# An attention stage rewritten: head products in pairs of 32-row tiles, one ring of bank pairs, the exp mask on GpSimd, head means out of the weights

## The chip, the core and the metric

The kernel runs on one core of a Trainium2 chip. The metric is the device time of one execution in microseconds: before, a median of 3298.95 over three runs (3294.93 to 3305.66). Times in the text are us unless marked ns.

## The reference

Four layers over x of 4 batches × 1,024 tokens × 128: causal attention, a mixture of experts, a message layer (sigmoid of products, 16 channels), and the same mixture again. Only attention is changed. Cut to it:

```python
x = x + attention(layernorm(x))                 # b, t, e = 4, 1024, 128; 16 heads of s = 8
k, q, v = (z @ Wk), (z @ Wq), (z @ Wv)          # each to (b, t, 16, 8)
k = layernorm(k over s) * kln_w + kln_b         # q likewise, with qln_w, qln_b
dot = einsum('bqhs,bkhs->bhqk', q, k) / sqrt(8)
dot = where(causal, dot, -inf)
out = einsum('bhqk,bkhs->bqhs', softmax(dot), v).reshape(b, t, e)
attention = out @ Wo + bo
```

## The kernel before

Phases follow each other with a barrier between: `setup_phase`, `attention_phase`, `moe_phase`, `message_phase`, `moe_phase`. In attention a **group** is 4 heads of one batch; 4 groups a batch, 16 in all. Tokens stand in 8 tiles of 128. Each head has a stack of 32 rows (`STACK`): high part of q or k, low part, high part again, and two rows for the shift by the row's maximum. Four stacks make 128 rows. `q_st` and `k_st` hold them by token; TensorE transposes them (L367) to `qT`, `kT`, `qmT` with tokens along the free dimension. Since one product must see one head only, `kT` has a copy of 1,024 columns for each head with zeros in the other heads' rows (`spread_keys`, L816 on VectorE for the first half, L577 on ScalarE for the second), and every product runs over all 128 rows.

A group does two passes over its scores. **Maxima** (one group ahead): TensorE makes q·k for a tile of queries (L390), adds the causal mask with a product of identity and mask (L393) into one of four 512-column banks `unit`, and VectorE reduces it (L823), 43 units a group. Then the **shift** (L831 to L835) puts minus the maximum into `q_st`, which is transposed again to `qmT`. **Scores**: for a tile j of keys, TensorE makes k·q shifted (L413), adds the mask (L416) into one of two banks `score`, and ScalarE takes exp into `prob` (L616), 43 units a group. **Weighing**: one step j behind, the values times `prob` go to `o_acc` (L435), fp32, in four 32-column tiles, one a head, side by side. After step 7 ScalarE copies `o_acc` to `oT` (L605), TensorE transposes it back (L449), VectorE divides by the sums (L845, L846). At a batch's end come the transposes of `o_tok`, the product with Wo (L532), and the addition to x (L922, L924, L929).

While one batch's groups run, the next batch is prepared: token statistics (L685), z (L695), its transposes, projection (L381), copies on ScalarE (L560, L561), means of heads, centring, squares, variance, scaling, weight and bias (L715 to L743) and stacks (L747 to L804) on VectorE.

The order is written out by hand in `program`: scores of step j, `beside` places maxima units between them by `max_slice`, then weighing of step j - 1. TensorE executes in that order. Two counters run for the banks, one for `score`, one for `unit`; a unit is filled when the unit before it in the same bank has been emptied:

```python
def wait_empty(self, eng):
    eng.wait_ge(unit_free[self.n % BANKS], self.b * (UNITS_BATCH // BANKS) + self.n // BANKS + 1)
```

Batch 0 is prepared ahead of the loop, the loop `Fori` runs batches 0 to 2, and the last batch stands behind it. GpSimd only clears buffers in this stage; SyncE clears rows in DRAM for the next stage.

## Time and profile before

| | |
|---|---|
| median of 3 runs | 3298.95 |
| profiled execution | 3302.05 |
| its span, instructions | 3300.3, 58108 |
| TensorE busy, weight loads | 2977.8, 1822.9 |
| VectorE, ScalarE, GpSimd | 1919.3, 1469.5, 546.5 |
| attention: first score product, last copy of `o_acc`, last statistics | 104.3, 894.4, 904.2 |
| longest waits from 104 to 900: ScalarE's exp for the mask product L416 | 178.0 |
| the same, for the score product L413 | 77.4 |
| TensorE's weight load of a score for ScalarE's exp | 86.5 |

The span is that of one execution. Busy time counts an instruction from start to end; TensorE's products overlap, so their busy time holds the tails of the last ones, and the distance from one start to the next tells what one costs in a row. "PEld" is the load of the stationary operand. "L413" is a line of the kernel; a helper's line stands for all its calls.

### The profile page before, as it was taken

The page shows a single profiled execution, that of the slowest core. Times are in us where ns is not written, and L with a number is a line of the kernel's source. Part 1 is how long each engine was busy: PE and PEld are TensorE (multiplying, and loading weights), DVE is VectorE, ACT ScalarE, POOL GpSimd, SP SyncE. Part 2 cuts the span into 40 slices and gives each one's busy share as a digit, 9 for nine tenths or more (in the row PEclk, how much of TensorE's full clock was granted, in tenths as well). Part 3 has the DMA queues.
Part 4 walks back from the last instruction along what each step waited for, and adds up shares of the span by engine and source line. Part 5 has one row for each costly group of instructions (what it writes and reads, how often), then busy time and mean ns, then how long its engine had stood idle before and what let it go on. Part 6 is the DMA issues. An engine that isn't in the chain of part 4 may idle for free. (4 is left out here: it accounts for less than half of the span.)

```text
span 3300.3 us, 58108 instructions
## 1 busy us (share of the span) xinstructions
PE 2977.8 (90%) x19154; PEld 1822.9 (55%) x19155; DVE 1919.3 (58%) x3658; ACT 1469.5 (45%) x2438; POOL 546.5 (17%) x577
## 2 busy tenths in 40 slices
PE   2898998989868995999999999999999999966997
PEld 1455555555466883555555555555555555545886
DVE  5696776866356674545455555555455544546666
ACT  1455555555544443444444444444444444424443
POOL 1000000000065431111111111111111111135732
PEclk8998998999968997999999999999999999976999
DMA  9000000000032313888888888888888888842222
GB/s 159 1 1 2 1 1 2 1 1 1 6 97 62 87 40 98 198 198 201 199 189 196 201 200 196 193 197 200 195 200 194 198 195 200 199 119 75 64 69 79
DMA packets 202940, 389.02 MB, mean 118 GB/s; under 512 B 44562, under 2 KB 117147, under 8 KB 198555
## 3 DMA queue, kind: packets, MB, share of 16 engines
q1 hardware_dynamic: 193562, 367.95, 48.4%
q0 software_dynamic: 9216, 19.02, 1.7%
q8 instruction: 88, 1.44, 0.2%
q14 instruction: 74, 0.60, 0.1%
HBM read 35.23 MB, written 31.75 MB: 20 GB/s over the span
## 5 line engine op out<-in xcount | busy, mean ns | idle before, releaser
L2019 DVE STREAM_TRANSPOSE m_turned<-m_sig 128x1024 f32<-128x1024 f32 x512 | 613.1, 1226 | 597.2 <-ACT m_sig L1932 576.2
L1932 ACT ACTIVATE m_sig<-m_f_ps 128x1024 f32<-128x1024 f32 x512 | 496.4, 1021 | 609.2 <-PE m_f_ps L1804 609.2
L1817 PE MATMUL m_v_ps<-m_sig,m_tok 128*64 128x512 f32 x2048 | 497.0, 606 | 0.0
L1829 PE MATMUL m_v_ps<-m_sigT,m_tok 128*64 128x256 f32 x4096 | 465.8, 380 | 7.5 <-DMA m_sigT<-m_turned 7.4
L616 ACT ACTIVATE a_prob<-a_score 128x512 f32<-128x512 f32 (+3 forms) x688 | 346.1, 528 | 263.8 <-PE a_score L416 178.0
L1804 PE MATMUL m_f_ps<-m_swap,m_own 64*128 64x512 f32 x1536 | 442.8, 421 | 12.0 <-DMA m_swap<-m_own 9.8
L1804 PE MATMUL m_f_ps<-m_own,m_swap 64*128 64x512 f32 x1536 | 442.9, 421 | 0.0
L823 DVE TENSOR_REDUCE a_maxima<-a_unit 128x1 f32<-128x512 f32 (+5 forms) x688 | 373.9, 597 | 95.2 <-PE a_unit L393 67.5
L1829 PEld LDWEIGHTS m_v_ps<-m_sigT,m_tok 128*64 128x64 f32 x4096 | 293.6, 137 | 213.3 <-issue 71.2
L413 PE MATMUL a_score<-a_qmT,a_kT 128*128 128x512 f32 (+3 forms) x768 | 315.7, 436 | 44.4 <-ACT a_prob L616 26.3
L1804 PEld LDWEIGHTS m_f_ps<-m_swap,m_own 64*128 64x128 f32 x1536 | 270.5, 186 | 142.8 <-issue 86.1
L390 PE MATMUL a_unit<-a_kT,a_qT 128*128 128x512 f32 (+3 forms) x768 | 289.7, 412 | 15.7 <-issue 4.6
L1956 POOL TENSOR_TENSOR m_own<-m_uv,m_own 128x1024 fp32r<-128x1024 f32 x64 | 152.1, 2377 | 842.9 <-ACT m_own L1917 842.9
L1804 PEld LDWEIGHTS m_f_ps<-m_own,m_swap 64*128 64x128 f32 x1536 | 270.3, 186 | 3.6
L1817 PEld LDWEIGHTS m_v_ps<-m_sig,m_tok 128*64 128x64 f32 x2048 | 124.4, 136 | 239.7 <-issue 239.7
L413 PEld LDWEIGHTS a_score<-a_qmT,a_kT 128*128 128x128 f32 x768 | 153.5, 202 | 128.0 <-ACT a_prob L616 86.5
L1393 POOL TENSOR_SCALAR f_h<-x,f_mean,f_rstd 128x128 f32<-128x128 f32 x64 | 50.2, 802 | 911.0 <-DVE f_away L1550 911.0
L1405 POOL DMA_INDIRECT back_rows<-f_y_rows,f_goes_to x160 | 154.6, 966 | 244.5 <-DVE f_y_rows L1581 236.4
L390 PEld LDWEIGHTS a_unit<-a_kT,a_qT 128*128 128x128 f32 x768 | 154.4, 204 | 69.9 <-issue 41.3
L1922 ACT COPY m_tok<-m_unit 128x512 f32<-128x512 f32 x128 | 69.0, 590 | 250.1 <-PE m_unit L1788 250.1
L1251 PE MATMUL f_y_ps<-f_w_down,f_innerT 128*128 x1280 | 169.5, 275 | 1.7 <-DVE f_y_rows L1581 1.3
L2028 DVE COPY m_v1T<-m_v_ps 128x256 f32<-128x256 f32 x128 | 54.3, 424 | 194.4 <-PE m_v_ps L1829 194.0
(286 smaller groups left out, 4279.7 us busy)
## 6 DMA issues: line engine op xcount, KB each, us to landing
m_sigT<-m_turned SPq DMA_DIRECT2D x2048, 128.0 KB, 2.4
m_swap<-m_own SPq DMA_DIRECT2D x64, 512.0 KB, 4.4
m_swap<-m_own SPq DMA_DIRECT2D x64, 256.0 KB, 5.0
f_t_rows<-f_sent_rows SPq DMA_DIRECT2D x162, 65.0 KB, 1.8
f_sent_rows<-clear_rows SPq DMA_DIRECT2D x40, 260.0 KB, 8.1
f_h<-back_rows SPq DMA_DIRECT2D x8, 512.0 KB, 4.9
f_norm_all<-back_rows SPq DMA_DIRECT2D x8, 512.0 KB, 5.5
back_rows<-f_y_rows,f_goes_to POOLq DMA_INDIRECT x160, 2.3
```

The costliest lines, as they stand in the source:

```text
L390: mm = pe.matmul(o, qT[g % 2][:, qt * P:(qt + 1) * P], kT[g % 2][:, h, first:first + width], start=True, stop=not masked)
L413: mm = pe.matmul(out[:, at:at + q1 - q0], kT[g % 2][:, h, lo:lo + P], qmT[g % 2][:, q0:q1], start=True, stop=q0 > lo)
L616: act.activation(prob[step % 2][:, heads[0]:heads[-1] + 1, q0:q1], src, ACT.Exp).then_inc(prob_ready[s % 2], 1)
L823: dve.tensor_reduce(maxima[:, qt, heads[0]:heads[-1] + 1, part], src[:, 0:len(heads) * width].rearrange("p (h w) -> p h w", w=width), AX.X ...
L1251: mm = pe.matmul(y_ps[:, 0:DIM], innerT[p][:, ib * P:(ib + 1) * P], w_down[:, ds(e * INTER + ib * DIM, DIM)], start=(ib == 0), stop=(ib == ...
L1405: pool.indirect_dma_start(back_rows[n // HALF_NB][:, :], bass.IndirectOffsetOnAxis(ap=goes_to[n % UNROLL][:, :], axis=0), y_rows[n % RING] ...
L1804: mm = pe.matmul(f_ps[s][:, cols], tile_of(u[rows, :], j + s * SIDE), v[rows, cols], start=start, stop=stop)
L1817: mm = pe.matmul(v2_ps[h * RANK:(h + 1) * RANK, :], tok[p][:, j + s * SIDE, 0, :], sig[j % 2][s][:, h * HALF:(h + 1) * HALF], start=(j == ...
L1829: mm = pe.matmul(v1_ps[h * RANK:(h + 1) * RANK, g * 2 * P:(g + 1) * 2 * P], tok[p][:, jj, 1, :], sigT[g][:, :, 2 * h:2 * h + 2, jj, :].rea ...
L1932: act.activation(sig[j % 2][s][:, :], f_ps[s][:, :], ACT.Sigmoid).then_inc(sig_ready, 1)
L1956: pool.tensor_tensor(own_lo[p][:, :], uv32[:, :], own_hi[p][:, :].bitcast(F32), ALU.subtract).then_inc(lo_ready, 1)
L2019: dve.transpose(turned[g][:, :, q, :, :], sig[j % 2][s][:, :].rearrange("p (t j a) -> p j t a", j=4, a=STACK)).then_inc(turn_ready, 1)
```

## The change

`qT`, `kT`, `qmT` have one copy of 1,024 columns, and a head's product uses only its 32 rows: a 32 × 128 tile of the array. A unit is now two heads in a pair of banks, up to 2 × 512 columns, 24 units of scores and 24 of maxima a group; the two products of a unit stand in different rows and different banks. The two products with the mask follow a maxima unit on the diagonal as before, over 128 rows. For scores no mask is added; exp is taken of all, and GpSimd sets the entries above the diagonal of each 128 × 128 block to zero in `prob` (`keep`), before the weighing reads them. A one-column addition goes before each.

All units, with transposes and projections, go through one ring of three bank pairs (`pairs`), and `sequence` gives one order that all engines read. Copies of transposed stacks and of z are ScalarE's, 1,024 wide. The means over a head are taken out of Wq and Wk in the setup, so sums and centring are gone. Squares, scaling, weight and bias of the heads are GpSimd's. Stacks are made one group at a time.

```diff
@@ setup_phase, VectorE: means of the heads out of the weights
+            dve.wait_ge(attn_in, 64)
+            by_head = k["w_qkv"][:, 0:2 * DIM].rearrange("p (h s) -> p h s", s=HD)
+            dve.tensor_reduce(head_sums[:, :], by_head, AX.X, ALU.add).then_inc(centre, 1)
+            dve.wait_ge(centre, 1)
+            dve.scalar_tensor_tensor(out=by_head, in0=head_sums[:, :].unsqueeze(2).broadcast_to([P, 2 * HEADS, HD]), scalar=-1.0 / HD,
+                                     in1=by_head, op0=ALU.mult, op1=ALU.add)
@@ attention_phase: the order of one group, read by all engines
-        def max_slice(g, j):
-            ends = (0, 0, 8, 17, 26, 34, MAX_UNITS, MAX_UNITS, MAX_UNITS) if g + 1 < GROUPS else (0, 0, 0, 10, 20, 29, 37, MAX_UNITS, MAX_UNITS)
...
+        def sequence(g, prev, prep, follows):
+            begin, end, made = (6 if g == GROUPS - 1 else 2), 19, 0
+            for i in range(SCORE_UNITS):
+                yield "score", i
+                if follows and i in (begin - 2, begin - 1):
+                    yield "stack", i - begin + 2
+                if prev and i == 2:
+                    yield "weigh", TILES - 1
+                if prev and i == 4:
+                    yield "empty_out", 0
+                if follows and begin <= i <= end:
+                    upto = -(-24 * (i - begin + 1) // (end - begin + 1))
+                    for n in range(made, upto):
+                        yield "max", n
+                    made = upto
+                    if i == end:
+                        yield "shift", 0
+                if i > LAST_OF[0] and i in LAST_OF:
+                    yield "weigh", LAST_OF.index(i) - 1
+                if prev and i == 9:
+                    yield "turn_out", 0
+                if prev and g == 0 and i in (13, 17):
+                    yield ("turn_tokens", "project_out")[i == 17], 0
+                if prep and g == 1:
+                    if i < 3:
+                        yield ("token_stats", "token_dev", "token_norm")[i], 0
+                    if i in (6, 7):
+                        yield "turn_z", i - 6
+                    if i in (11, 13, 15, 17):
+                        yield "project", (i - 11) // 2
+                if prep and g == 2 and i in (1, 3, 5, 6, 7, 9, 12):
+                    yield {1: ("square", 1), 3: ("square", 0), 5: ("square_sums", 0), 6: ("head_dev", 0), 7: ("head_rstd", 0),
+                           9: ("affine", 1), 12: ("affine", 0)}[i]
+                if prep and g == 3 and i in (0, 21):
+                    yield "stack_heads", i // 21
+                if prep and g == 0 and prev and i in (12, 20):
+                    yield "stack_heads", 2 + i // 20
+                if follows and i == 21:
+                    yield "turn_shifted", 0
+        class Units:
@@ the ring
-        score = [ctx.enter_context(nc.psum_tensor(f"a_score{i}", [P, HALF], F32)) for i in range(2)]
-        unit = [ctx.enter_context(nc.psum_tensor(f"a_unit{i}", [P, HALF], F32)) for i in range(BANKS)]
+        pairs = [ctx.enter_context(nc.psum_tensor(f"a_pair{i}", [P, SEQ], F32)) for i in range(RINGS)]
+            def wait_empty(self, eng, *emptied):
+                latest = {n % RINGS: n for n in sorted((*emptied, self.n - RINGS)) if n >= 0}
+                for n in latest.values():
+                    self.wait_emptied(eng, n)
@@ TensorE
-                        mm = pe.matmul(o, qT[g % 2][:, qt * P:(qt + 1) * P], kT[g % 2][:, h, first:first + width],
-                                       start=True, stop=not masked)
+            def maxima_unit(u, g, n, stacks=()):
+                qt, pair, k0, k1, masked, _ = MAXES[n]
+                out = by_head(u.next(), k1 - k0)
+                u.wait_empty(pe, *stacks)
+                for i in range(2):
+                    rows = head_rows(2 * pair + i)
+                    mm = pe.matmul(out[:, i, :], qT[g % 2][rows, qt * P:(qt + 1) * P], kT[g % 2][rows, k0:k1], start=True, stop=not masked)
+                if masked:
+                    for i in range(2):
+                        mm = pe.matmul(out[:, i, k1 - k0 - P:k1 - k0], k["ident16"][:, :], k["mask"][:, :], start=False, stop=True)
+                mm.then_inc(unit_full, 1)
-                            mm = pe.matmul(out[:, at:at + q1 - q0], kT[g % 2][:, h, lo:lo + P], qmT[g % 2][:, q0:q1],
-                                           start=True, stop=q0 > lo)
-                            if q0 == lo:
-                                mm = pe.matmul(out[:, at:at + P], k["mask"][:, :], k["ident16"][:, :], start=False, stop=True)
+            def scores(u, g, n, shifted=()):
+                j, pair, q0, q1 = SCORES[n]
+                out = by_head(u.next(), q1 - q0)
+                u.wait_empty(pe, *shifted)
+                for i in range(2):
+                    rows = head_rows(2 * pair + i)
+                    mm = pe.matmul(out[:, i, :], kT[g % 2][rows, j * P:(j + 1) * P], qmT[g % 2][rows, q0:q1], start=True, stop=True)
+                mm.then_inc(unit_full, 1)
@@ ScalarE
+            def weights(u, n):
+                j, pair, q0, q1 = SCORES[n]
+                src = by_head(u.next(), q1 - q0)
+                u.wait_full(act)
+                act.activation(prob[j % 2][:, 2 * pair:2 * pair + 2, q0:q1], src, ACT.Exp).then_inc(u.free(), 1)
@@ GpSimd
+            def affine(nb, a):
+                one = qk[:, :, a, :, :]
+                pool.wait_ge(rstd_ready, nb + 1)
+                pool.tensor_tensor(one, one, qk_rstd[:, a, :, :].unsqueeze(3).broadcast_to(rows), ALU.mult).then_inc(scaled_done, 1)
+                for i in range(2):
+                    w = k["ln_rows"][:, (2 * a + i) * HD:(2 * a + i + 1) * HD].unsqueeze(1).unsqueeze(1).broadcast_to(rows)
+                    pool.wait_ge(scaled_done, 4 * nb + 2 * (1 - a) + i + 1)
+                    pool.tensor_tensor(one, one, w, (ALU.mult, ALU.add)[i]).then_inc((scaled_done, affine_done)[i], 1)
+            def keep(u, G, j, made):
+                u.wait_emptied(pool, made)
+                pool.tensor_tensor(steps[:, j:j + 1], ones_column, ones_column, ALU.add)
+                mine = prob[j % 2][:, :, j * P:(j + 1) * P]
+                pool.affine_select(out=mine, in_=mine, compare_op=ALU.is_ge, fill=0.0, base=0, pattern=[[0, GROUP], [1, P]],
+                                   channel_multiplier=-1).then_inc(kept, 1)
@@ VectorE: of the head work there remain
-                def head_sums(a):
-                def head_centred(a):
-                def head_squares(a):
-                def head_scaled(a):
-                def head_affine(a, i):
-                def spread_keys(g):
-                def empty_queries(dst, i):
...
+            def maxima_unit(u, n):
+                qt, pair, k0, k1, _, part = MAXES[n]
+                src = by_head(u.next(), k1 - k0)
+                u.wait_full(dve)
+                dve.tensor_reduce(maxima[:, qt, 2 * pair:2 * pair + 2, part], src, AX.X, ALU.max).then_inc(u.free(), 1)
```

TensorE in the first group of the loop, where scores of key tile 1 (384 columns) stand beside maxima; `a_score`, `a_unit` before and `a_pair` after are the banks, L413 of before and L429 of after are scores, L390 and L413 maxima, L393 and L416 masks. Before:

```order
L413 MATMUL a_score<-a_qmT,a_kT 128x512
L390 MATMUL a_unit<-a_kT,a_qT 128x384
L393 MATMUL a_unit<-mask,ident 128x128
L410 REGISTER_ALU
L413 MATMUL a_score<-a_qmT,a_kT 128x384
L416 MATMUL a_score<-ident,mask 128x128
```

After:

```order
L429 MATMUL a_pair<-a_qmT,a_kT 128x384 x2
L413 MATMUL a_pair<-a_kT,a_qT 128x256 x2
L416 MATMUL a_pair<-mask,ident 128x128 x2
L429 MATMUL a_pair<-a_qmT,a_kT 128x384 x2
L413 MATMUL a_pair<-a_kT,a_qT 128x384 x2
L416 MATMUL a_pair<-mask,ident 128x128 x2
```

One head and one mask a unit became two heads a row, with masks (two of them) only behind maxima.

TensorE from one group's end into the next; L367 of before and L384 of after are transposes of stacks, L435 and L447 the weighing. Before:

```order
L367 MATMUL a_unit<-ident,a_q_st 128x128 x8
L429 REGISTER_ALU
L435 MATMUL a_o_acc<-a_prob,a_v 32x128 x4
L336 REGISTER_ALU
L413 MATMUL a_score<-a_qmT,a_kT 128x512
L416 MATMUL a_score<-ident,mask 128x128
L413 MATMUL a_score<-a_qmT,a_kT 128x512 x2
L416 MATMUL a_score<-ident,mask 128x128
L367 MATMUL a_unit<-ident,a_q_st 128x128 x4
L367 MATMUL a_unit<-ident,a_k_st 128x128 x4
```

After:

```order
L384 MATMUL a_pair<-ident,a_q_st 128x128 x8
L429 MATMUL a_pair<-a_qmT,a_kT 128x128 x4
L447 MATMUL a_o_acc<-a_prob,a_v 32x256 x4
L509 UNCONDITIONAL_BRANCH
L509 ISA
L429 MATMUL a_pair<-a_qmT,a_kT 128x512 x2
L404 ISA
L384 MATMUL a_pair<-ident,a_q_st 128x128 x8
L429 MATMUL a_pair<-a_qmT,a_kT 128x512 x2
L354 REGISTER_ALU
L384 MATMUL a_pair<-ident,a_k_st 128x128 x8
```

The transposes of a stack went from two units of four to one of eight, and the next group's first score now stands behind one unit of shifted queries and two narrow score units.

GpSimd in the group that prepares the heads; L648 is a mask (128 × 4 × 128), L637 and L641 scaling, weight and bias. After (before has nothing there):

```order
L646 TENSOR_TENSOR a_steps<-ones 128x1
L648 AFFINE_SELECT a_prob<-a_prob 128x4x128
L636 REGISTER_ALU
L637 TENSOR_TENSOR a_qk<-a_qk,a_qk_rstd 128x8x128
L640 ISA
L641 TENSOR_TENSOR a_qk<-a_qk,ln_rows 128x8x128
L640 REGISTER_ALU
L641 TENSOR_TENSOR a_qk<-a_qk,ln_rows 128x8x128
L637 TENSOR_TENSOR a_qk<-a_qk,a_qk_rstd 128x8x128
L640 REGISTER_ALU
L641 TENSOR_TENSOR a_qk<-a_qk,ln_rows 128x8x128
```

Three of the six 1,024-element products on q and k are seen; the mask of the next step stands behind all six.

## Rows read from the trace of the kernel before

**Rows 1.** Of the page, busy time of each engine.
```profile
PE 2977.8 (90%) x19154; PEld 1822.9 (55%) x19155; DVE 1919.3 (58%) x3658; ACT 1469.5 (45%) x2438; POOL 546.5 (17%) x577
```

**Rows 2.** Stretches: start:end, us, busy time (x instructions) of each engine, granted clock, DMA share, GB/s.
```profile
15.00:104.00 89.00, 34.68 (x128) 21.68 (x128) 66.45 (x106) 10.09 (x26) 9.99 (x5) 0.82 0.75 120
104.00:303.00 199.00, 183.23 (x1172) 103.72 (x1173) 147.10 (x275) 113.07 (x220) 0.00 (x0) 0.95 0.00 1
```

**Rows 3.** Waits from 104 to 900 us: who for whom, us in total, times, longest.
```profile
ACT a_prob L616 <- PE a_score L416: 178.0, 170, 3.1
```

**Rows 4.** Order in time from 400 us: start, us, engine, line, instruction.
```profile
405.56 0.47 PE L390 MATMUL a_unit<-a_kT,a_qT 128*128 128x512 f32 x1
...
406.22 0.34 PE L413 MATMUL a_score<-a_qmT,a_kT 128*128 128x384 f32 x1
...
406.44 0.47 PE L390 MATMUL a_unit<-a_kT,a_qT 128*128 128x512 f32 x1
```

**Rows 5.** Order in time from 1600 us, the message stage.
```profile
1603.22 0.39 PE L1804 MATMUL m_f_ps<-m_swap,m_own 64*128 64x512 f32 x1
1603.22 0.39 PE L1804 MATMUL m_f_ps<-m_own,m_swap 64*128 64x512 f32 x1
...
1603.45 0.39 PE L1804 MATMUL m_f_ps<-m_swap,m_own 64*128 64x512 f32 x1
...
1603.92 0.39 PE L1804 MATMUL m_f_ps<-m_swap,m_own 64*128 64x512 f32 x1
...
1604.24 0.20 PEld L1817 LDWEIGHTS m_v_ps<-m_sig,m_tok 128*64 128x64 f32 x4 [0.36 <-issue]
...
1604.43 1.94 ACT L1932 ACTIVATE m_sig<-m_f_ps 128x1024 f32<-128x1024 f32 x2 [0.31 <-PE m_f_ps L1804]
```

**Rows 6.** Groups of instructions by form, whole span: shapes, count, busy us, mean ns, idle before.
```profile
L1932 ACT ACTIVATE m_sig<-m_f_ps 128x1024 f32<-128x1024 f32 x512 | 496.4, 1021 | 609.2 <-PE m_f_ps L1804 609.2
...
L823 DVE TENSOR_REDUCE a_maxima<-a_unit 128x1 f32<-128x512 f32 x384 | 249.9, 682 | 37.9 <-PE a_unit L390 19.8 <-PE a_unit L393 14.1
...
L823 DVE TENSOR_REDUCE a_maxima<-a_unit 128x1 f32<-128x128 f32 x64 | 18.1, 283 | 4.8 <-PE a_unit L393 4.1
...
L616 ACT ACTIVATE a_prob<-a_score 128x128 f32<-128x128 f32 x64 | 17.5, 273 | 37.9 <-PE a_score L416 37.9
...
L715 DVE TENSOR_REDUCE a_qk_sum<-a_qk 128x128 f32<-128x1024 f32 x8 | 9.7, 1215 | 8.8 <-ACT a_v_next L561 8.7
```

**Rows 7.** Order in time from 292.5 us, the end of the first batch.
```profile
292.84 1.06 PE L435 MATMUL a_o_acc<-a_prob,a_v 128*32 128x512 f32 x8
...
293.84 0.50 PE L390 MATMUL a_unit<-a_kT,a_qT 128*128 128x512 f32 x1
...
294.18 0.23 PE L393 MATMUL a_unit<-mask,ident 128*128 128x128 bf16 x1
...
301.46 1.02 ACT L605 COPY a_oT<-a_o_acc 128x1024 f32<-128x1024 f32 x1
...
302.54 1.09 PE L449 MATMUL a_unit<-ident,a_oT 128*128 128x128 f32 x8 [1.23 <-ACT a_oT L605]
303.23 0.26 DVE L845 RECIPROCAL a_o_den<-a_unit 128x16 f32<-128x16 f32 x1 [1.99 <-PE a_unit L449]
```

**Rows 8.** Groups by form on GpSimd, whole span.
```profile
L1956 POOL TENSOR_TENSOR m_own<-m_uv,m_own 128x1024 fp32r<-128x1024 f32 x64 | 152.1, 2377 | 842.9 <-ACT m_own L1917 842.9
...
L162 POOL TENSOR_SCALAR_AFFINE_SELECT ident<-ident 128x128 f32<-128x128 f32 x1 | 0.3, 285 | 0.2 <-POOL mask L160 0.2
```

**Rows 9.** Order in time from 31 and from 353 us, preparing of a batch.
```profile
31.17 2.14 DVE L695 TENSOR_SCALAR a_z<-x,a_mean,a_rstd 128x128 f32<-128x128 f32 x8
...
353.60 1.45 PE L381 MATMUL a_unit<-w_qkv,a_zT 128*128 128x384 f32 x4
```

**Rows 10.** Stretches, columns as in rows 2.
```profile
83.00:98.00 15.00, 13.11 (x49) 7.14 (x47) 15.00 (x31) 0.00 (x0) 0.00 (x0) 1.00 0.00 1
320.00:330.00 10.00, 7.83 (x36) 5.26 (x37) 5.89 (x17) 5.74 (x10) 0.00 (x0) 0.60 0.00 1
```

More of the change, by code:

```diff
@@ new lines, in _ @@
+            u = Units(0, 0)
+            token_dev(0)
+            for i in range(2):
+                empty_z(u, i)
+            made = [projected(u, i) for i in range(4)]
+            head_dev(0)
+            values(u, made[1:])
+            for i in range(2):
+                empty(u, (qT, kT)[i][0])
+            u.n += len(MAXES)
+            empty(u, qmT[0])
+            group(u, 0, 0, False, False, True)
+            with act.Fori(0, BATCH - 1) as b:
+                u = Units(b, UNITS_BEFORE)
+                made = group(u, b, 1, True, True, True)
+                for g in (2, 3):
+                    group(u, b, g, True, True, True)
+                group(u, b + 1, 0, True, True, True, made[1:])
@@ new lines, in _ @@
+            u = Units(0, 0)
+            for made in range(3, 6):
+                u.wait_emptied(pool, made)
+            for a in (1, 0):
+                square(0, a)
+            for a in (1, 0):
+                affine(0, a)
+            u.n += UNITS_AHEAD
+            group(u, 0, 0, False, False, True)
+            with pool.Fori(0, BATCH - 1) as b:
+                u = Units(b, UNITS_BEFORE)
+                made = group(u, b, 1, True, True, True)
+                group(u, b, 2, True, True, True, made)
+                group(u, b, 3, True, True, True)
+                group(u, b + 1, 0, True, True, True)
@@ L667, in _ @@
+            b, u = BATCH - 1, Units(BATCH - 1, UNITS_BEFORE)
+            for g in (1, 2, 3):
+                group(u, b, g, True, False, g < GROUPS - 1)
         @block.vector
@@ new lines, in _ @@
+            link, u = Link(dve, link_sem), Units(0, 0)
+            token_stats(link, 0)
+            token_norm(link, 0)
+            u.n += 6
+            square_sums(link, 0)
+            head_rstd(0)
+            for g in range(GROUPS):
+                stack_heads(link, 0, g)
+            u.n += 2
+            for n in range(len(MAXES)):
+                made = maxima_unit(u, n)
+            shift(u, link, 0, made)
+            u.n += 1
+            group(u, link, 0, 0, False, False, True)
@@ L938, in attention_phase @@
+            for g in (1, 2, 3):
+                group(u, link, b, g, True, False, g < GROUPS - 1)
+            normalise(u, link, GROUPS - 1)
+            u.next()
+            add_out(u, link, b)
         phase.close()
```

851 lines of the change are left out of this document (327 added, 524 removed).

## The prediction

> **What bounds the kernel now.** I read the page's busy shares first, then the stretches by stage, the waits of the attention stage, and last the order in time. The page [rows 1] says TensorE 90% of the span, VectorE 58%, ScalarE 45%. The change touches the attention stage and adds two instructions to the setup, so the stretches count [rows 2]: before 104 us TensorE does 35 us of 89; from there it is busy 183 us in a batch of 199, VectorE 147, ScalarE 113, GpSimd nothing. The stage ends about 905 us into the span of 3300.3. Its 16 head groups, from 104 to 894, take 49.4 us each, the preparing of the next batch included. Mostly the others wait for TensorE: 178 us in [rows 3] are ScalarE waiting for a mask product. Behind 905 us the program is the same, and I leave it as it is.
>
> Busy is not full, though [rows 4]: from 405.56 to 406.44 TensorE issues two 512-column maxima products, one 384-column score product and a mask behind each kind. That is 0.88 us for 1,408 columns and two masks. At the 0.234 us for 512 columns found below, the columns need 0.64, so a mask costs 0.12. A group has 36,864 columns of products (16.9 us), 64 masks (7.7), 9.6 of weighing and 3.4 of transposes: 38 us of issue in 49.4, before preparing. The rest is waiting and the tails of products.
>
> **The change, part by part.** *Products in pairs.* Two heads' products stand in different 32-row tiles and different banks. Before does not show 32-row tiles of an attention product, but the message stage has pairs of 64-row tiles, 512 columns [rows 5]: both start together, and the next pair 0.23 us later (1603.22, 1603.45). I take 0.234 us for a pair, the nearest row; the bounds are 0.22 and, if 32-row tiles went one after the other, 0.47. A group has 24 score pairs and 24 maxima pairs. In columns each set is 9,216 (half of 18,432), 4.2 us at 0.234 a 512, about 5 with some 0.03 us of floor on narrow ones. Score masks go: 32 products a group. Maxima masks stay: 16 units with two mask products. Each also leaves the row tiles and comes back. The row shows 0.32 us from the last pair to the next stage's first product instead of 0.234, so 0.09 a switch; two masks at 0.05 to 0.1 and two switches make 0.32 us a unit (bounds 0.2 and 0.5), 5.1 a group. Probabilities times values are untouched: 0.99 us for 512 columns of four heads (292.84 to 293.84 in [rows 7]), 9.6 us a group. Four sets of eight transposes are 0.85 each (1.09 less the tail [rows 7]), 3.4. TensorE's issue is then 5 + 5 + 5.1 + 9.6 + 3.4 = 28 us a group, 10 less than the 38 above.
>
> The Trainium skill, TensorEngine Tiling (Array Packing), Key Properties, says that changing the tiling mode drains the engine. That speaks against row tiles between full-size masks: with a whole tail (0.39 less 0.234, 0.16 us in the pair's row) for each of the 32 new switches, the group grows by 2 us, and the time by some 33 us. The row shows 0.09, so I stay with that.
>
> *VectorE.* 24 reductions replace 43, twice as wide. From 283 ns for 128 and 683 for 512 [rows 6] the slope is 1.04 ns an element; 1,024 give 1.21 us, as a 1,024 reduction already takes [rows 6]. 4 × 0.42 + 4 × 0.68 + 4 × 0.95 + 12 × 1.21 = 22.7, less 0.05 overlap each, 21.5 a group. Spreading of keys and queries goes to ScalarE, head means go, squares and affine go to GpSimd: 37 us a group becomes about 27.
>
> *ScalarE.* An exp of 1,024 is 1.02 us (the sigmoid of the same shape), of 128 0.27 [rows 6], 0.107 for each 128 more: 24 (12 of 1,024, 4 each of 768, 512 and 256) make 19.2. Full-width copies of queries, keys, shifted queries and output make 4.1. Some 25 a group, 28 now.
>
> *GpSimd.* A mask of 512 elements a step; 128 elements take 0.285 [rows 8]. If that is all fixed cost, it is 0.3, if it is all per element, 1.14; I take 0.7. One step lies between the exp and the product that needs it, over 1 us, so nothing. In the group that prepares heads, six 1,024-element products of 2.4 us [rows 8] stand in GpSimd's queue ahead of mask 3: 14.3 us from about 12.6 us into the group puts it near 27.6, and the weighing that wants it is due at 25. 2 us a batch, none to 6.
>
> *The ring.* No engine has more than 28 us in a group, so what sets the pace is who waits for whom. Scores and maxima now share one ring of three pairs, and TensorE, in order, may fill unit n only when unit n-3 is empty. A filled unit reaches its reader 0.27 us after its issue ends (1603.92 + 0.23 to 1604.43 [rows 5]; half of eight transposes, 302.54 + 0.41 to 303.23 [rows 7]), and a freed one restarts TensorE 0.06 to 0.08 later (301.46 + 1.02 to 302.54 [rows 7]). I stepped one middle group through this with the durations above, from its first maxima pair at 0: the first weighing (2.0 us) starts at 7.4 us, the second at 15, the third at 21, the fourth at 25, the last reduction ends at 29.3. A piece of it: behind the first weighing, at 9.4, score 8 issues to 9.5 and maxima 8 and 9 to 10.0; score 9 waits for exp 8 until 10.3; reductions 8 and 9 run from 10.0 to 12.3, and the output transposes wait for the second of them. VectorE stands idle 7 us of it, mostly behind weighings of 1.3 to 2 us while the ring holds 1.0 to 1.2 us of work. Then nothing overlaps: shift 0.65, eight transposes 1.1, copy 1.02, two narrow exps 0.7, exp 1.0, copy of queries 1.02, exp 1.0, copy of keys 1.02, 0.1: 7.7 us until the next maxima pair. 37 us. Ten restarts a group with an exposed weight load (0.34 from 293.84 to 294.18 [rows 7] instead of 0.24) add 1, so 38.
>
> *The clock.* TensorE now has a granted clock of 1.00 or near in most of the stage, and 0.60 behind a batch's start, where it waits [rows 10]. With more waiting I take 0.85 for the stage: 30% at 1.2 GHz, on 28 us of work 8 us, of which a quarter is not hidden, 2. So 40 us a group; bounds 36 and 45.
>
> *Preparing a batch.* Projections are 4 units of two products, 1.28 each (1.45 less a tail of 0.17 [rows 9]), and z transposes 0.9 on TensorE; z takes VectorE 2.1 [rows 9]; the statistics fall into its idle time: 8. Square sums 2 × 1.21 and a reciprocal on VectorE: 3, and the late mask 2. Output transposes 0.85 and projection 1.7 (eight times a third of 0.64), two additions of 1.21 and eight statistics: 3. 16 a batch; bounds 8 and 25.
>
> *Start and end.* Up to 104 the head work moves to GpSimd at twice the price (squares 4.8, affine 14.3) but means and centring go, and VectorE stacks four groups ahead of its first maxima: 26.7 us where 26.5 are now. 0, bounds -5 and +8. The tail has the same chain, 12 us. The setup's two reductions lie beside loads.
>
> **Sum.** 104 + 38 (first group) + 3 × (4 × 40 + 16) + 2 × 40 + 24 (the last group has no maxima; ScalarE's exps bound it) + 12 = 786 us where the stage now ends at 905. 119 us less. The profiled execution took 3302.05 us, 3 over the median of 3298.95: 3183 there, 3180 against the median.
>
> **Rivals.** *Row tiles do not run together, or switches cost twice.* Then each hop carries 0.24 us more and TensorE 8 us: 45.5 a group, stage end about 871, 3265. For: 32 rows are not 64. Against: [rows 5].
> *The engines overlap almost fully.* A group is then 24 + 7.7 us, preparing 14: end about 655, 3050. For: 28 us of TensorE is the largest sum. Against: a ring of three with 1 us units.
> *The clock falls.* The mechanism of the other side: TensorE waits so often in the ring that it stays at 1.2 GHz. Its 28 us double, 10 of that is hidden: 57 us a group, with preparing 20 the stage ends at 1059, 3455: 273 us over the forecast if throughout, 3365 at two thirds. The 119 us in hand are gone at 44% of it. For: 0.60 from 320 to 330, behind the waits of a batch's start. Against: between 83 and 98 us TensorE fed VectorE at its pace with gaps at each unit and was granted 1.00 [rows 10]. The Trainium skill, TensorE: Matmul & The Clock Gate, in its section on psum-queue depth-cycling, describes just this swing between the levels in a kernel that cycles PSUM banks; the row from 83 to 98 does not agree, the one from 320 does.
> *GpSimd's masks are late everywhere.* At 1.3 us and more with the queue before them, each late weighing costs up to 1 us, 3 a group: 3230.
> That the change doesn't do what it says I exclude: the order shown above has two products a unit, and GpSimd's masks.
>
> **Chances and range.** The forecast 0.62, own range 3125 to 3240; late masks 0.07, no overlap of tiles 0.13, full overlap 0.11, clock 0.07. The bounds of a group, 36 to 45 for 16 groups, with preparing from 8 to 25, would be 3090 to 3285. A range of 3095 to 3255 leaves out most of the full overlap, half of the no-overlap case and the clock, 2 in 10. A difference of 0.3% (10 us) is what can be told from none. Of the no-overlap case 0.10 is still faster, 0.02 same and 0.01 slower; of the clock case 0.01 is same and 0.06 slower. So faster 0.90, same 0.03, slower 0.07.
>
> **What would show it.** Pairs of attention products starting within 0.02 us and 0.23 apart; about 40 us between copies of the output; VectorE near 60 to 65% busy in the stage, waiting for TensorE as TensorE waits for exp and reduction; gaps of VectorE of 8 to 9 us once a group; mask 3 behind GpSimd's affine. Wrong: pairs 0.47 apart, a granted clock under 0.75, or one engine over 90% busy.

## The result and the profile after

| | median of runs | profiled execution | span | granted clock |
|---|---|---|---|---|
| before | 3299.62 us (3294.93 to 3305.66, 4 runs) | 3302.05 us | 3300.3 us | 0.948 |
| after | 3269.65 us (3262.68 to 3278.11, 4 runs) | 3278.11 us | 3276.4 us | 0.891 |

The ratio is 0.9918, with a 95% interval of 0.9898 to 0.9937: 30 us less, where 119 were forecast. Run again, the same two kernels gave 0.9897 (0.9880 to 0.9914). Most of it is in the attention stage: between the two profiled executions the span is 24 us shorter, and the stage's last statistics start at 887.7 us instead of 904.2 (at 872.1 in the second execution of after). The forecast had them at 786.

First the page's row of TensorE's busy time and its clock row by slices, in tenths; the attention stage is the first eleven slices of 82 us.

```profile
PE 2931.8 (89%) x18642; PEld 1710.9 (52%) x18643; DVE 1759.5 (54%) x3206; ACT 1418.6 (43%) x2072; POOL 715.3 (22%) x865
...
PEclk7676777766769997999999999999999999976998
```

Then stretches of after, columns as in [rows 2]: the start, the first batch, a plain group (from one output copy to the next), and the stretch between the last two output copies. By "plain group" I mean here and below the period from the second to the third output copy of the stage, and the same one of the next two batches; it holds little preparing, but not none: GpSimd's scaling of the heads and some 6 us of VectorE.

```profile
15.00:104.00 89.00, 38.58 (x147) 22.71 (x148) 38.37 (x87) 14.74 (x21) 26.95 (x13) 0.67 0.77 120
104.00:303.00 199.00, 178.81 (x1061) 77.90 (x1059) 108.24 (x159) 101.59 (x131) 42.90 (x74) 0.71 0.00 1
...
207.40:250.90 43.50, 39.03 (x238) 16.90 (x237) 28.10 (x37) 24.34 (x31) 20.28 (x23) 0.71 0.00 1
854.40:873.90 19.50, 16.66 (x140) 5.83 (x138) 0.78 (x2) 14.29 (x21) 5.38 (x14) 0.85 0.00 1
```

VectorE fell from 147 to 108 us in the first batch, as wanted. But the granted clock, 0.95 there before [rows 2], is 0.71, and TensorE's busy time hardly fell (183.2 to 178.8 us). The same group in before:

```profile
209.10:253.60 44.50, 42.46 (x288) 23.90 (x288) 37.35 (x66) 25.33 (x50) 0.00 (x0) 1.00 0.00 1
```

So a plain group went from 44.5 us at 2.4 GHz to 43.5 with 0.71 granted. The clock has the two levels 1.2 and 2.4 GHz, so that is 58% of the time at 1.2 GHz. What that level costs shows best in the stretch where nothing overlaps. In time order (start, us, engine, line), score pairs with eight transposes between them, first at 2.4 GHz, then at 1.2:

```profile
293.94 1.09 PE L384 MATMUL a_pair<-ident,a_q_st 128*128 128x128 f32 x8
...
296.13 0.50 PE L429 MATMUL a_pair<-a_qmT,a_kT 32*128 32x512 f32 x2 [0.27 <-ACT a_qmT L555]
296.56 1.09 PE L384 MATMUL a_pair<-ident,a_q_st 128*128 128x128 f32 x8
297.59 0.49 PE L429 MATMUL a_pair<-a_qmT,a_kT 32*128 32x512 f32 x2
...
299.04 0.50 PE L429 MATMUL a_pair<-a_qmT,a_kT 32*128 32x512 f32 x2
...
300.59 0.33 PE L413 MATMUL a_pair<-a_kT,a_qT 32*128 32x128 f32 x2 [0.70 <-ACT a_kT L555]
...
352.72 0.79 PE L429 MATMUL a_pair<-a_qmT,a_kT 32*128 32x512 f32 x2 [1.87 <-issue]
353.44 1.97 PE L384 MATMUL a_pair<-ident,a_q_st 128*128 128x128 f32 x8
355.34 0.79 PE L429 MATMUL a_pair<-a_qmT,a_kT 32*128 32x512 f32 x2
...
357.96 0.79 PE L429 MATMUL a_pair<-a_qmT,a_kT 32*128 32x512 f32 x2
```

A step takes 1.46 us in the one and 2.62 in the other. The waits of the stage, answering to [rows 3] (there 178.0 us):

```profile
ACT a_prob L561 <- PE a_pair L429: 299.8, 182, 4.4
DVE a_maxima L743 <- PE a_pair L416: 238.3, 144, 10.6
```

Both readers wait for TensorE, more than before, and TensorE is busy 39.0 of 43.5 us: by the page alone one would say that it is short of time. The experiments say what it is short of.

### The profile page after: what moved, and what is told of

Its sections match the earlier page's. It is cut to its first block and busy times, and to the rows that moved or that the text cites. A ratio compares the mean times of both kernels' runs of the same rounds, so it can differ in the third digit from the quotient of the medians.

```text
span 3276.4 us, 55735 instructions
## 1 busy us (share of the span) xinstructions
PE 2931.8 (89%) x18642; PEld 1710.9 (52%) x18643; DVE 1759.5 (54%) x3206; ACT 1418.6 (43%) x2072; POOL 715.3 (22%) x865
## 5 line engine op out<-in xcount | busy, mean ns | idle before, releaser
L743 DVE TENSOR_REDUCE a_maxima<-a_pair 128x2 f32<-128x1024 f32 (+3 forms) x384 | 354.7, 953 | 304.4 <-PE a_pair L416 240.2
L561 ACT ACTIVATE a_prob<-a_pair 128x1024 f32<-128x1024 f32 (+3 forms) x384 | 303.3, 815 | 308.8 <-PE a_pair L429 299.8
L429 PE MATMUL a_pair<-a_qmT,a_kT 32*128 32x512 f32 (+3 forms) x768 | 193.5, 544 | 40.2 <-ACT a_prob L561 17.7
L413 PE MATMUL a_pair<-a_kT,a_qT 32*128 32x512 f32 (+3 forms) x768 | 188.4, 549 | 40.7 <-DVE a_maxima L743 17.7
L447 PE MATMUL a_o_acc<-a_prob,a_v 128*32 128x512 f32 (+3 forms) x1536 | 219.8, 692 | 5.3 <-POOL a_prob L648 4.9
L429 PEld LDWEIGHTS a_pair<-a_qmT,a_kT 32*128 32x128 f32 x768 | 79.7, 224 | 194.3 <-issue 115.2
L646 POOL TENSOR_TENSOR a_steps<-ones 128x1 f32<-128x1 f32 x128 | 25.5, 200 | 655.3 <-ACT a_prob L561 655.3
```

Source lines behind the costliest of these rows:

```text
L413: mm = pe.matmul(out[:, i, :], qT[g % 2][rows, qt * P:(qt + 1) * P], kT[g % 2][rows, k0:k1], start=True, stop=not masked)
L429: mm = pe.matmul(out[:, i, :], kT[g % 2][rows, j * P:(j + 1) * P], qmT[g % 2][rows, q0:q1], start=True, stop=True)
L447: mm = pe.matmul(o_acc[h * STACK:(h + 1) * STACK, q0:q1], v1[:, j, g * GROUP + h, :], prob[j % 2][:, h, q0:q1], start=(j == 0), stop=(j == ...
L561: act.activation(prob[j % 2][:, 2 * pair:2 * pair + 2, q0:q1], src, ACT.Exp).then_inc(u.free(), 1)
L743: dve.tensor_reduce(maxima[:, qt, 2 * pair:2 * pair + 2, part], src, AX.X, ALU.max).then_inc(u.free(), 1)
```

## The experiments

Theories: **clock by rows**, the 32-row products leave TensorE at 1.2 GHz and that costs some 6 us a group; **clock by waiting**, the forecast's own wording, TensorE pauses too often; **ring**, the walk through three bank pairs sets the pace whatever the clock; **queue**, for the preparing of a batch (below). Each ratio is to before on the same chip. Chips differ by up to 3% in the total: before took 3387, 3388 and 3393 us beside some of these runs (two chips), 3297 and 3303 beside the others (two more). The difference is not in this stage: the run with full rows had its last output copy at 815.4 and 815.1 us on two chips, with 3309 and 3226 us in all. So I compare ratios and places in the stage, above all the time of the last output copy (before 894.4, after 873.9 and 858.3 in two executions, 16 us apart) and the plain group, of which each stage has three. The table gives the lowest and highest of the three and the clock granted in them; TensorE's busy share there was 0.90 in after and in full_rows, 0.95 to 0.96 in same_rows, 0.84 to 0.86 in half_rows.

| run | ratio (95%) | last copy, us | plain groups, us | granted there |
|---|---|---|---|---|
| before | 1 | 894.4 | 44.5 to 44.6 | 1.00 |
| after | 0.9918 (0.9898-0.9937) | 873.9 | 43.5 | 0.70 to 0.71 |
| after, again | 0.9897 (0.9880-0.9914) | 858.3 | 43.5 | 0.70 to 0.71 |
| zeros_1 | 1.0166 (1.0121-1.0212) | 947.5 | 50.4 to 59.0 | 0.57 to 0.73 |
| zeros_2 | 1.0064 (1.0042-1.0086) | 918.4 | 45.6 to 46.4 | 0.90 to 0.93 |
| two_pairs | 1.0700 (1.0677-1.0724) | 1123.9 | 58.7 to 59.9 | 0.61 to 0.65 |
| full_rows | 0.9759 (0.9739-0.9780) | 815.4 | 40.4 | 1.00 |
| same, second chip | 0.9770 (0.9753-0.9786) | 815.1 | 40.4 | 1.00 |
| same_rows | 1.0396 (1.0374-1.0418) | 1027.5 | 50.6 to 55.7 | 0.59 to 0.67 |
| half_rows | 0.9792 (0.9775-0.9809) | 824.4 | 38.7 to 41.3 | 0.88 to 0.92 |
| same, second chip | 0.9775 (0.9752-0.9798) | 817.7 | 38.7 to 40.3 | 0.89 to 0.91 |
| half_zeros | 0.9910 (0.9881-0.9940) | 862.0 | 42.4 to 42.5 | 0.92 |
| half_zeros_all | 0.9960 (0.9945-0.9974) | 882.5 | 43.9 to 46.2 | 0.86 to 0.89 |
| late_alone | 0.9887 (0.9856-0.9919) | 854.5 | 43.0 to 43.6 | 0.70 |
| half_late | 0.9777 (0.9756-0.9799) | 821.2 | 40.1 to 41.3 | 0.88 to 0.91 |
| spread_alone | 0.9833 (0.9809-0.9856) | 839.0 | 43.5 to 43.7 | 0.70 |
| heads_on_dve | 0.9987 (0.9971-1.0003) | 885.6 | 49.8 to 50.0 | 0.67 to 0.68 |
| half_spread | 0.9714 (0.9695-0.9733) | 797.2 | 38.7 to 40.3 | 0.89 to 0.92 |
| same, second chip | 0.9693 (0.9679-0.9707) | 794.8 | 38.9 to 40.3 | 0.89 to 0.91 |
| half_spread_q | 0.9724 (0.9710-0.9738) | 807.8 | 37.8 to 40.4 | 0.87 to 0.91 |

**More work on TensorE (zeros_1, zeros_2).**

```
+    def add_zeros(n):      # behind each score (and, in zeros_2, maxima) unit while the sum is open
+        for _ in range(n):
+            pe.matmul(o_acc[:, HALF:SEQ], zeros16[:, :], some16[:, :], start=False, stop=False)
...
```

> The kernel after, with one more product on TensorE behind each score pair for as long as bank two of the sum is open (19 a group): zero weights times 512 columns of bf16, added to that bank, so it changes no number. The clock theory (half of the attention stage runs at 1.2 GHz because TensorE pauses at each of the 48 units, and a plain group of 43.5 us has 59% of its time at that level): the granted clock of 104 to 885 us rises from about 0.7 to over 0.8, a plain group falls to 39 to 41.5 us, the whole to 3200 to 3240. The ring theory (three pairs in turn and the readers' time set the pace, the clock only stretches products that lie beside it): the clock may rise, a plain group stays at 43.5 or grows by up to 19 x 0.2 = 4 us, the whole 3270 to 3330.

> As the run with one product of zeros, but also one behind each maxima pair in the same stretch (35 a group, some 7.5 us of TensorE at 2.4 GHz, 15 at 1.2). Clock theory: granted clock near 1 in the groups, a plain group 37 to 40 us, the whole 3170 to 3230; with less gain than the first only if the added issue now stands in the ring's way. Ring theory: a plain group 44 to 50 us, the whole 3280 to 3380.

Both came out slower. The larger dose is where the ring theory had it, in the group and in the total; the smaller is worse than either theory allowed. The larger dose brought the clock up, 0.93 in the plain group:

```profile
221.80:267.50 45.70, 44.03 (x272) 18.54 (x277) 28.31 (x37) 24.45 (x31) 19.93 (x23) 0.93 0.00 1
```

35 products of 512 columns are 7.5 us at 2.4 GHz; 43.5 + 7.5 would be 51.0, and 45.7 was measured. If the products cost their whole length, 5.3 us came back with the clock; if some of them filled idle time, less did, so 5.3 is an upper estimate. The products cost more than they bought. The smaller dose was not enough: two of the three plain groups went to 59.0 us at 0.57, for a reason that no run shows.

**The ring (two_pairs).** The edit is `RINGS = 3` to `RINGS = 2`.

> The kernel after with a ring of two bank pairs instead of three. Ring theory: a walk of 48 units takes 3/2 of its waits; 38 us of ring at full clock become some 50 to 57, the whole 3480 to 3580. Clock theory with the ring not binding (TensorE's own stretched products the limit): under 48 us a group, the whole under 3350. The granted clock should be lower still than after's under both, since TensorE pauses longer.

```profile
243.50:303.40 59.90, 47.50 (x235) 19.25 (x235) 28.09 (x37) 24.81 (x31) 19.39 (x22) 0.61 0.00 1
```

16.4 us more a group, 250 in the stage; the ratio is inside the ring theory's range, the group above its 50 to 57. The ring sets the pace, as the forecast said, and its 0.61 shows that more waiting goes with a lower clock too.

**Rows at work (full_rows, same_rows).** In the products of `maxima_unit` and `scores`:

```
-    rows = head_rows(2 * pair + i)      # 32 rows, two tiles together
+    rows = slice(0, P)                  # full_rows: 128 rows, one after the other
+    rows = head_rows(2 * pair)          # same_rows: 32 rows, one after the other
```

> The kernel after with the row tiles alone undone: the two products of each score and maxima unit take all 128 rows instead of 32, so they can't run together (it leaves out keeping the heads apart: both halves of a unit hold the sum over the four heads). If row tiles are what the clock dislikes (a 32-row product counting for less work): the granted clock returns to 0.9 and more, and a plain group costs 43.5 - 5 + 48 x 0.13 (mean width of 288 columns at 2.4 GHz) = about 45, the whole 3270 to 3300. If pairs in one go are worth what the forecast put on them and the clock stays as low: a plain group 49 to 52 us, the whole 3360 to 3410.

> The kernel after, but both products of each score and maxima unit use the first head's 32 rows, so they take turns on one row tile (it leaves out the second head of each pair: the first stands twice). It has the serial products of the run with full rows, but 32 rows of the array at work instead of 128. If the number of rows at work is what holds the granted clock up: the clock stays at 0.6 to 0.75 in the stage and a plain group takes 46 to 52 us. If only the time that TensorE is occupied counts: it looks like the run with full rows, clock over 0.9 and a plain group of 40 to 41 us.

```profile
200.10:240.50 40.40, 36.26 (x243) 20.56 (x241) 27.87 (x37) 24.23 (x31) 19.76 (x22) 1.00 0.00 1
```

```profile
232.10:282.80 50.70, 48.13 (x238) 23.68 (x239) 28.54 (x37) 24.61 (x32) 19.69 (x22) 0.67 0.00 1
```

This pair decides it. The two kernels issue the same number of products with the same columns in the same order, and the two of a unit never run together (a score and a maxima product of different heads sometimes do in same_rows). With 128 rows TensorE was granted 1.00, with 32 rows 0.67 (0.59 in the next two batches), though it was busy 95% of that group against 90%. Busy time is not what kept the clock up here, and waiting is not what brought it down first: after itself is busy 90% of its plain group, as full_rows is, at 0.71. With the row tiles undone, the core of the change, the stage is faster than after's, and the plain group of 40.4 us is 4.6 below the 45 that was expected of it. But full_rows is a measurement, not a kernel to use: it leaves out keeping the heads apart, and a correct kernel with 128 rows would have to spread the keys again, as before did.

A rival is that going from row tiles to 128 rows and back, which full_rows does not do at all, is what lowers the clock. The next version goes back and forth as often as after.

The Trainium skill, TensorE: Matmul & The Clock Gate, section Part 1: The HAM clock gate, has the gate follow how busy the engine has been. These two runs do not agree with that if busy is counted as the profile counts it: the busier one had the lower clock.

**Both at once (half_rows).** A pair is heads p and p+2, in two 64-row tiles; the keys are kept twice, with the other head's rows zero.

```
-    rows = head_rows(2 * pair + i)
+    rows = slice(64 * i, 64 * i + 64)
+    act.activation(kT[..][:, 0, ..], src[..], ACT.Copy, scale=one_of[:, 0:1])       # heads 0 and 2
+    dve.tensor_scalar(kT[..][:, 1, ..], src[..], one_of[:, 1:2], None, ALU.mult)    # heads 1 and 3
...
```

> A version that computes everything: a pair is heads p and p+2, each product takes 64 rows (its own head's 32 and 32 rows of zeros in the keys), so two run together and fill all 128 rows. The keys are kept twice (one copy by ScalarE, one by VectorE, both scaled by a column of ones and zeros, in halves that take turns on the banks: about +0.4 us a group on the stretch without overlap). If rows at work (zeros included) hold the clock: granted 0.9 and more, a plain group 38 to 40.5 us, ratio to before 0.960 to 0.978. If the pairs' being together is what lowers the clock (TensorE less of the time at work): clock at 0.7, a plain group 43.5 to 45, ratio 0.99 to 1.01.

```profile
204.70:245.00 40.30, 33.87 (x242) 15.92 (x242) 28.06 (x37) 24.25 (x31) 19.91 (x23) 0.92 0.00 1
```

0.9792 on one chip and 0.9775 on another, at the upper edge of the 0.960 to 0.978 that the clock theory gave, and clear of the 0.99 to 1.01 of the other. Rows of zeros held the clock up as well, at a busy share of 0.84, so the going back and forth does not explain after's 0.71. What pairs in one go are worth at 2.4 GHz shows in the period between the 14th and the 15th output copy, which holds no preparing at all. In a later version of this kernel that differs from it only in preparing (half_spread, below) it was granted 1.00, in both executions. That version, then half_rows, then full_rows:

```profile
743.60:778.00 34.40, 29.54 (x229) 13.00 (x228) 22.06 (x26) 20.28 (x28) 6.19 (x16) 1.00 0.00 1
```

```profile
768.80:805.20 36.40, 31.87 (x228) 13.80 (x228) 22.12 (x26) 20.41 (x27) 6.22 (x16) 0.91 0.00 1
```

```profile
758.50:796.20 37.70, 34.93 (x229) 19.03 (x228) 21.89 (x26) 20.47 (x27) 6.19 (x16) 1.00 0.00 1
```

34.4 us in pairs, 36.4 (half_rows itself) at 0.91, and 37.7 with full rows in turn; after needs 41.9 at 0.70. Pairs together are worth 3.3 us a group at the same clock, and by this estimate a plain group of after would be 40.4 - 3.3 = 37.1 at full clock. No run shows after itself at that level.

**Zeros in the serial stretch (half_zeros, half_zeros_all).** 12 products of zeros a group there, or 19 spread over it.

> The version with 64-row products, and two products of zeros (512 columns, all 128 rows and columns of the array) behind each of the scores 20 to 23, 0 and 1 of a group: the stretch in which only exps, copies and transposes alternate (12 a group, 2.6 us of TensorE at 2.4 GHz). Clock theory: the 17% of a plain group at 1.2 GHz go to under 5%, a plain group 38.7 to 40.2 becomes 37 to 38.5, the preparing groups gain more, ratio to before 0.965 to 0.976. Ring theory: TensorE has nothing to do there but what the next copy waits for, so the zeros delay it, +0 to +2.6 us a group: 0.979 to 0.992.

> The version with 64-row products and one product of zeros behind each score while the sum is open (19 a group, 4 us). On after, the same dose raised the granted clock little and cost 52 us. Clock theory: the share at 1.2 GHz falls to under 5%, but part of the zeros stands in the ring's way: 38 to 41 us a plain group, ratio 0.970 to 0.985. If a product of zeros costs its whole length wherever it stands: 42.5 to 44 a plain group, ratio 0.995 to 1.005.

Both missed the clock theory's numbers and met the other's: 38 and 58 us later at the last copy than half_rows. The 188 products of half_zeros in the trace, at 0.21 us, are 40 us: in the serial stretch they cost their whole length, and the clock in a plain group did not rise (0.92 in both kernels). The 52 us that the second text gives for this dose on after are against before; against after's last copy it was 74 us.

**Preparing a batch.** After pays 26 to 35 us a batch above four plain groups in the first execution and 24 to 27 in the second, and I had said 16. A first guess was one root that ScalarE reaches too early.

```
-    if i < 3: yield ("token_stats", "token_dev", "token_norm")[i], 0
+    if i in (0, 4, 5): yield {0: "token_stats", 4: "token_dev", 5: "token_norm"}[i], 0
...  # and turn_z at i 8 and 9 instead of 6 and 7
```

> The kernel after with one thing moved: the square root for the next batch's token statistics stands behind the fifth exp of group 1 instead of the second, z behind the sixth, the z transposes two scores later. In after, ScalarE reaches that root while VectorE is still at the statistics it needs, and every exp behind it waits; then two table loads of 1.28 us stand in the stretch in which nothing overlaps. If that wait is why preparing a batch costs 30 to 35 us and not 16: 4 to 6 us less in each of three batches, 12 to 18 us in all, 3250 where after took 3267, ratio 0.984 to 0.987. If the wait only takes the place of another: within 4 us of after.

> The same move in the version with 64-row products. There the group behind a batch's start took 57 us against 39 of a plain one, and VectorE waited 2.8 us, ScalarE 3 us around the root. If the wait costs its length: 12 to 18 us less than 64-row products alone, ratio 0.974 to 0.976. By the other theory the ratio stays at 0.979.

The guess fell: 0.9887 against 0.9897 is no difference, and half_late's 0.9777 against 0.9792 and 0.9775 is none either. The trace of after shows a larger wait in the group behind a batch's start:

```profile
339.26 1.22 DVE L769 TENSOR_TENSOR a_proj<-a_pair,bo_rows 128x1024 f32<-128x1024 f32 x1 [1.09 <-PE a_pair L465]
...
340.65 1.23 DVE L772 TENSOR_TENSOR x<-x,a_proj 128x1024 f32 x1 [0.16 <-DVE a_proj L769]
342.03 1.48 DVE L774 BATCH_NORM_STATS2 stats<-x  x6 [0.15 <-DVE x L772]
...
344.24 2.34 DVE L743 TENSOR_REDUCE a_maxima<-a_pair 128x2 f32<-128x1024 f32 x2
345.50 0.59 PE L429 MATMUL a_pair<-a_qmT,a_kT 32*128 32x256 f32 x4 [3.07 <-DVE a_maxima L743]
```

On VectorE the residual addition and its statistics stand before two reductions; TensorE waits 3.07 us for the first of them, and ScalarE, behind it, 4.3. So I moved these, the spreading of one group's heads, and the root:

```
+    if prev and g == 0 and i == 22: yield "add_rest", 0     # x += proj and its statistics, was at 17
-    stack_heads at (g 3: 0, 21), (g 0: 12, 20)         # in words
+    stack_heads at (g 3: 0, 21, 22), (g 0: 20)
...
```

> The same three moves in the kernel after, with nothing else. Queue theory: last copy 12 to 20 us before after's 859 to 874, ratio 0.982 to 0.986. TensorE theory: ratio 0.988 to 0.992.

> 64-row products, and three moves of VectorE's and ScalarE's preparing work: the square root of the token statistics three scores later, the residual addition and its eight statistics (3.3 us) from the middle of group 0 to its end, the spreading of a group's keys and queries (2.1 us) from there to the end of group 3; all where VectorE stands idle while exps, copies and transposes alternate. If preparing costs 28 us a batch because such work stands in VectorE's queue before reductions that the ring waits for: 5 us and more less in each of three batches, last copy at 800 to 810, ratio 0.969 to 0.975. If preparing costs that through TensorE and the ring (projections 4 x 1.6, z and output transposes, the output projection, fewer scores to spread the maxima over): within 4 us of 64-row products alone, ratio 0.977 to 0.981.

0.9833 and 0.9714, both where the queue theory had them, with the last copies at 839.0 and 797.2. The same group before and after the moves, without any change of products (after in its second execution, then spread_alone):

```profile
296.90:354.80 57.90, 44.91 (x285) 20.84 (x284) 36.99 (x77) 27.23 (x34) 6.41 (x16) 0.74 0.01 2
```

```profile
296.50:347.80 51.30, 42.76 (x282) 20.66 (x280) 33.09 (x61) 24.49 (x31) 6.74 (x16) 0.77 0.01 2
```

Preparing is then 15 to 21 us a batch, where the second execution of after had 24 to 27: the queue theory holds for about 6 us of it. Some of the fall between these two lines is work that moved over the group's edge. As the root alone did nothing, the 6 us belong to the other two moves; no run separates them.

**Head work back on VectorE (heads_on_dve).** `square` and `affine` issued by VectorE at the same places of the order.

> The kernel after with one part of the change undone: the squares and the affine of keys and queries are VectorE's again (8 instructions of 1,024 elements a batch at some 1.2 us, 9.7 us) instead of GpSimd's. The forecast counted the move as part of the gain. If VectorE's queue decides: +5 to +10 us a batch, at the start some -7 (1.2 us instead of 2.4 each), in all +10 to +20, ratio 0.992 to 0.996. If VectorE's idle time (it has 22 us of reductions in 43.5) takes it, and the start gains: -5 to -15, ratio 0.985 to 0.988.

```profile
199.20:249.00 49.80, 40.10 (x237) 17.23 (x238) 35.67 (x44) 24.22 (x32) 7.18 (x16) 0.67 0.00 1
```

0.9987, slower than either theory allowed: this part of the change alone is worth 0.9% of the kernel. The head work falls into just the period that I call a plain group. VectorE is busy 36 of 50 us there, and still it grows by 6.3 us: idle time is not time at the right place. At the start it is the reverse, the first copy comes 7 us earlier (148.1 against 155.1 in the second execution of after).

**The serial stretch (half_spread_q).** VectorE instead of ScalarE copies the transposed queries.

> 64-row products and the three moves, and the copy of the transposed queries from PSUM by VectorE instead of ScalarE. In the stretch between the last reduction and the next maxima, ScalarE alone does five steps of 1 us in series (shifted queries, exp, queries, exp, keys), VectorE one half of the keys. If that series is what the stretch waits for: 1 us less a group, less where VectorE has preparing there (two of four), 8 to 15 us of 3202 in all, ratio 0.967 to 0.970. If TensorE's transposes and pairs between are the series, or the copy arrives no sooner: within 3 us, ratio 0.970 to 0.973.

Missed: 0.9724 beside 0.9693 for its base on the same chip, not faster but 0.3% slower. The rows of steps above suggest why: at 2.4 GHz a step of 1.46 us is TensorE's own pair (0.43 until the transposes start) and eight transposes (1.03), so a free ScalarE changes nothing; and VectorE's copy is 1.23 us where ScalarE's was 1.01. This is argued from after's trace, not shown by a run.

half_spread is the fastest version found: 0.9714 and 0.9693 of before, about 3202 us where before took 3297.

## Why the prediction was wrong

- **What bounds.** Right that the others wait for TensorE and that waits, not busy shares, set the pace. two_pairs shows the ring.
- **The ring walk, 38 us.** As far as can be told right: 37.1 is the estimate at full clock, 40.4 was measured with the products in turn. The stretch without overlap is 7.3 us at 2.4 GHz (shift 0.65, then from 293.94 to 300.59), forecast 7.7.
- **Prices.** Right in the main: reductions of 1,024 took 1.22 us, exps 1.03, masks of GpSimd 0.65 (0.7 taken), and TensorE waited 4.9 us for its masks in the whole stage. The last group took 24.3 us from its first score (849.6) to the last output copy, forecast 24. The masks of a maxima unit with their two switches of row tiles hold too: at 2.4 GHz the masks start 0.33 to 0.43 us behind a 512-column pair, 0.10 to 0.20 more than the 0.23 taken for the pair, and the next pair 0.21 behind the masks, 0.31 to 0.41 us in all where the forecast had 0.32. The parts are different ones, though: full_rows, which does not switch, has 0.09 from the masks to the next product, so the two switches together cost 0.22 to 0.32 us, up to the whole tail (0.16) for each that the forecast decided against, and the masks are cheaper than it thought. After, then full_rows on the second chip:

```profile
205.07 0.28 PE L416 MATMUL a_pair<-mask,ident 128*128 128x128 bf16 x2
205.28 0.50 PE L429 MATMUL a_pair<-a_qmT,a_kT 32*128 32x512 f32 x2
```

```profile
106.63 0.28 PE L416 MATMUL a_pair<-mask,ident 128*128 128x128 bf16 x2
106.72 0.60 PE L429 MATMUL a_pair<-a_qmT,a_kT 128*128 128x384 f32 x2
```

- **The clock.** This is the step that failed. The text took 0.85 for the stage and "of which a quarter is not hidden, 2" us a group. The stage had 0.72 (0.76 in the second execution), a plain group 0.71, and the cost is, by the estimate above, 43.5 - 37.1 = 6.4 us. Over fourteen groups that makes 3.5 us each beyond the forecast's 40: 49 us. The rival "The clock falls" (0.07) had the level right but not the cause: it put it on waiting, and full_rows, with the same share of waiting as after, was granted 1.00. I had dismissed it with [rows 10], a stretch at 1.00 with gaps at each unit; but those products had 128 rows. The forecast counted columns and waits, and nowhere that each product would use a quarter of the array. Nor did the rival's size fit: its 57 us a group assumed TensorE's 28 us doubled with 10 hidden, and that all the time.
- **Preparing, 16 a batch.** Mis-sized: 24 to 35, 28 to 41 us in all beyond the forecast. "The statistics fall into its idle time" was argued from sums; spread_alone shows some 6 us a batch of such work standing in the ring's way. Before already paid 28, 30 and 15 us a batch, counted the same way (the first: 47.7 + 47.9 + 66.0 less three groups of 44.5), which I did not work out from its trace.
- **Start.** 0 forecast, with bounds -5 and +8. The first score starts at 99.3 instead of 104.3, although the granted clock up to 104 us is 0.67 instead of 0.82. The head work on GpSimd costs 9 us there (the first score of heads_on_dve starts at 90.9, that of the second execution of after at 99.9), so the rest of the change gave back some 14; no run separates its parts.
- **The sum.** The last copy stands at 873.9 where the forecast's sum has 774, 100 us later. By the first scores of the groups: the start is 5 us earlier, the first group 46.5 us instead of 38, the twelve groups with preparing 611.5 instead of 528, the next two 92.3 instead of 80, the last as forecast. The clock's 49 and the 41 of preparing are 90 of it; what the first group and those two have beyond that stays open.
- **Rivals.** Row tiles do run together, so that one is out; full overlap and late masks too. Of the signs of being wrong, "a granted clock under 0.75" came true, with 0.72, though narrowly, as the second execution has 0.76.

What else stays open: why half_rows has about 0.90 in most groups, and its later version 1.00 in one of them, and how much of the 24 to 35 us belongs to projections and transposes, which no run left out.

## What to carry to other kernels

Before packing small products into row tiles, ask what granted clock the unpacked ones had. If it was 1.00, price the packed version at 1.2 GHz as well, in every series that runs through TensorE; here two 64-row tiles with rows of zeros kept most of the packing and most of the clock, which made them about as fast as full rows in turn (0.978 to 0.979 against 0.976 to 0.977), with the heads kept apart. And work preparing out of the trace of the kernel before (its periods less a plain period): what stands in an engine's queue before the instruction that a ring waits for can cost its length, however idle the engine is on average.

## What the hardware showed unexpectedly

- 32-row products in turn were granted 0.67, the same products with 128 rows 1.00, at 95% and 90% busy; two 64-row tiles together, half of their key rows zero, 0.92 at 84%.
- Going back into row tiles behind two mask products took 0.21 us where staying with 128 rows took 0.09.
- Four 32-row tiles run together, not only the two of a unit: a score pair and a maxima pair, two products each, start 0.01 us apart.

```profile
264.51 0.79 PE L429 MATMUL a_pair<-a_qmT,a_kT 32*128 32x512 f32 x2
264.52 0.79 PE L413 MATMUL a_pair<-a_kT,a_qT 32*128 32x512 f32 x2
```

- Too few products of zeros made it worse than none or many: groups of 50.4 to 59.0 us at 0.57 to 0.73, against 43.5 at 0.71 and 45.7 at 0.93.
- The same kernel's time differs by up to 3% between chips, in the part behind this stage.
